# Expert layer: tokens routed and stored in four groups into a fixed region per expert, expert tiles fetched from computed addresses

## The chip, the core and the metric

The kernel runs on one core of a Trainium2 chip. The time is device time of one execution in microseconds (us), the median of several runs. Five engines work beside each other: TensorE (PE: matrix products; its weight loads show as PEld), VectorE (DVE), ScalarE (ACT), GpSimd (POOL) and SyncE (SP), which here only issues DMA transfers. They wait for each other by semaphores alone.

## The reference, cut to what matters

A stack of six layers over 64 x 32 = 2048 tokens of 256 numbers. Five of them (three kinds of attention, a ternary feed-forward layer and a gated attention) are left as they are. The sixth is a mixture of eight experts with a top-2 choice, whose inputs and weights are quantised:

```python
def activation_quant(x):                       # per token
    scale = 127.0 / jnp.maximum(jnp.max(jnp.abs(x), axis=-1, keepdims=True), EPS)
    return jnp.clip(jnp.round(x * scale), -128.0, 127.0) / scale
def expert_ffn(x, gw, uw, dw):                 # 256 -> 512 -> 256
    gate = bitlinear(x, gw)
    up = bitlinear(x, uw)
    activated = up * jnp.square(jax.nn.relu(gate))
    return bitlinear(activated, dw)
...
# last layer: x is normalised, a softmax over x @ router_w.T gives 8 probabilities a token,
# the two largest are kept and divided by their sum; the token's output is
# weight_1 * expert_1(x) + weight_2 * expert_2(x), and it is added to x
```

## The kernel before, in words

All layers stand in one program; each engine runs its own instruction list, layer after layer. The change is in the last layer, `experts` (L2437), and in one transfer of an earlier layer's list.

Tokens are held as 16 tiles of 128 (one token a partition). Each token goes to two experts, so 4096 rows have to be sorted by expert. Sorted, they fill at most `TILES` = 40 tiles of 128 rows, each of one expert, with blank rows at the end of an expert's last tile. The sorting goes through a table in device memory, `row_store`, of 40 x 128 rows of `ROW` = 132 words: 128 words hold the 256 quantised numbers as pairs of 16-bit floats, the last four the token's scale, its weight and the place its result goes to (`f_goes`). The stages are, with their engines:

- **Normalise and measure.** DVE normalises tile by tile (L165, `f_xn`) and takes each token's largest absolute value (L2657), from which the scales follow (L2663 to L2666). The whole of this comes first, for all 16 tiles.
- **Logits.** PE turns two tiles at a time (`turn_x`, L2798), ACT copies them out (`turned`, L2577), PE multiplies by the router's weights (`route`, L2806); all logits lie in one bank of PSUM.
- **Round and pack.** ACT rounds each tile to integers (`rounds`, L2582), POOL copies the low half words into `f_rows`, twice, since each token has two rows (L2550, 16 copies).
- **Route.** DVE takes softmax, ranks and choices of all 2048 tokens at once (L2681 to L2696, operations of 128 x 1024 among them), and "takes" of each token's two experts a value by multiplying by a mask and adding (`take`, L2699 and L2700). PE counts how many rows each expert gets and each row's rank within its expert (L2820 to L2824), with ACT's copy of the counts between (L2602). DVE makes of these counts the first tile of each expert, and from that each row's slot, `f_index`.
- **Store.** POOL issues 32 indirect DMAs (L2558), each of 128 rows to the slots that `f_index` gives; it waits ahead of the first for all copies, all scales, all indices and for the transfer that had written blank rows over the table (`f_blank_stored`; SP issues it at L857, in the second layer, on the queue that also brings the weights).
- **Fetch and compute.** SP waits for all 32 stores and then fetches the table in 20 sets of two tiles (L2532), up to six ahead. For each set PE turns the rows (`turn_in`, L2835), multiplies by up, gate and down weights whose place it reads from `f_owner_i` (L2878), ACT and DVE do what lies between, DVE takes the hidden rows' largest values and scales (L2747 to L2753), and POOL stores the results by indirect DMA (L2564, two a set) to `f_y_store`. At the end SP reads both results of each token back, they are added, and the output is stored.

SP, POOL and each compute engine do their list in order; a DMA issue that waits holds everything behind it on its engine. The lines of the kernel that the change touches:

## Time and profile before

| | |
|---|---|
| median of 3 runs (2062.59 to 2067.57) | 2063.86 us |
| the profiled execution: its own time | 2064.5 us |
| the profiled execution: span of the trace | 2061.7 us |
| mean granted TensorE clock | 0.924 |
| PE busy | 1688.7 us (82%) |
| DVE busy | 1586.4 us (77%) |
| ACT busy | 1190.8 us (58%) |
| POOL busy | 601.3 us (29%) |

Times in the trace count from the start of the span, so the last layer, which begins at about 1845 us, is read with times of 1845 to 2061.7. The busy shares are means over six layers; the change touches the last one alone, and what counts there is which wait ends last. The profiled execution's own time is 2.8 us above its span and 0.64 us above the median.

### The profile page before, as it was taken

To read this page: it belongs to the slowest core of one execution; us is meant where nothing else is said; L and a number is where in the kernel's file an instruction comes from. 1 tells how busy PE (TensorE), PEld (TensorE's weight loads), DVE (VectorE), ACT (ScalarE), POOL (GpSimd) and SP (SyncE) were. 2 spreads that over 40 slices of the span, in tenths; PEclk is the share of its full clock that TensorE was granted. 3 is DMA by queue.
4 is the path that set the end of the run, shared out by engine and by line. 5 is a ranking of instruction groups with operands and counts; after the bars stand their busy time and mean duration, and the time that the engine had idled before them with its cause. 6 is when DMAs were issued, how large, how long until landed. Compare 5 with 4: busy or idle time off the path is not lost.

```text
span 2061.7 us, 45477 instructions
## 1 busy us (share of the span) xinstructions
PE 1688.7 (82%) x13802; PEld 1240.8 (60%) x13802; DVE 1586.4 (77%) x4308; ACT 1190.8 (58%) x3322; POOL 601.3 (29%) x734
## 2 busy tenths in 40 slices
PE   6999999999999979766569898989899688862373
PEld 4677777777777758533357666666677566652241
DVE  5688888888888858789748878888887288873496
ACT  2555566556655636456427666676767466642493
POOL 0022222222222201011123434444433154435342
PEclk9999999999999999879779999999999789965797
DMA  2011111111111141020021222222111100000124
GB/s 97 15 33 29 29 29 29 29 29 29 30 32 29 43 107 24 32 79 1 3 70 43 62 62 62 62 62 62 41 32 33 25 14 12 12 11 20 52 76 154
DMA packets 119516, 87.10 MB, mean 42 GB/s; under 512 B 76992, under 2 KB 95747, under 8 KB 118661
## 3 DMA queue, kind: packets, MB, share of 16 engines
q1 hardware_dynamic: 116484, 79.71, 14.8%
q0 software_dynamic: 2944, 6.37, 0.9%
q8 instruction: 38, 0.62, 0.1%
q14 instruction: 50, 0.40, 0.1%
HBM read 72.05 MB, written 12.21 MB: 41 GB/s over the span
## 4 chain that ended last, share of the span: by engine, by line
PE 37%; DVE 30%; issue 15%; ACT 11%; POOL 2%; DVEq 1%; DMA 1%; ACTq 1%; SPq 1%; POOLq 0%
PE ps L669 3%; PE ps L1967 3%; PE ps L691 3%; PE ps L1895 3%; ACT a_pr L403 2%; DVE a_pT L532 2%; DVE a_nm L524 2%; PE ps L737 2%; DVE d_ks L1764 2%; PE ps L1946 2%; PE ps L1905 2%; PE ps L707 2%; ACT d_pr L1698 1%; POOL f_row_store L2558 1%; PE ps L1958 1%
## 5 line engine op out<-in xcount | busy, mean ns | idle before, releaser
L403 ACT ACTIVATE a_pr<-ps,a_nm 128x257 f32<-128x257 f32 x512 | 238.1, 473 | 174.3 <-DVE a_nm L524 174.3
L532 DVE COPY a_pT<-ps 128x512 f32<-128x512 f32 x256 | 170.3, 686 | 60.0 <-PE ps L707 59.5
L1718 ACT ACTIVATE d_pr<-d_st,d_nm 128x257 f32<-128x257 f32 x256 | 128.1, 502 | 128.7 <-DVE d_nm L1827 127.4
L330 POOL TENSOR_TENSOR a_sf<-a_sf,a_ratio 128x256 f32<-128x256 f32 x64 | 39.5, 616 | 474.1 <-DVE a_ratio L553 474.1
L524 DVE TENSOR_REDUCE a_nm<-ps 128x2 f32<-128x514 f32 x256 | 174.5, 681 | 0.0
L707 PE MATMUL ps<-ident,a_pr 128*128 128x128 f32 x1024 | 159.0, 278 | 0.0
L1946 PE MATMUL ps<-d_kc,d_qc 128*128 128x257 f32 x512 | 141.9, 400 | 14.7 <-DVE d_vc L1803 14.7
L1626 POOL TENSOR_TENSOR d_kc<-d_kc,d_ks 128x257 f32<-128x257 f32 x64 | 60.2, 941 | 266.4 <-ACT d_dist L1683 130.6
L707 PEld LDWEIGHTS ps<-ident,a_pr 128*128 128x128 f32 x1024 | 120.6, 143 | 25.7 <-issue 12.7
L669 PE MATMUL ps<-a_cT,a_wqk 128*128 128x257 f32 x512 | 132.7, 381 | 1.9 <-ACT a_v L393 0.8
L678 PE MATMUL ps<-a_wvg,a_cT 128*128 128x256 f32 x512 | 127.6, 392 | 0.0
L1631 POOL TENSOR_TENSOR d_qc<-d_qc,d_qs 128x512 f32<-128x512 f32 x64 | 94.2, 1472 | 81.6 <-DVE d_qs L1775 81.6
L1946 PEld LDWEIGHTS ps<-d_kc,d_qc 128*128 128x128 f32 x512 | 90.9, 191 | 42.9 <-DVE d_vc L1803 17.3
L1698 ACT ACTIVATE d_pr<-d_pr,d_ri 128x257 f32<-128x257 f32 x256 | 114.6, 497 | 0.0
L678 PEld LDWEIGHTS ps<-a_wvg,a_cT 128*128 128x128 f32 x512 | 92.0, 189 | 34.7 <-issue 24.8
L1823 DVE CUSTOM_DVE_ANT_0 d_st<-ps,d_wm 128x257 f32<-128x257 f32 x256 | 98.7, 424 | 15.1 <-issue 7.8
L691 PE MATMUL ps<-a_kT,a_qbd 32*128 32x289 f32 x1024 | 98.5, 453 | 13.2 <-ACT a_pr L403 10.3
L1691 ACT ACTIVATE d_pT<-ps 128x512 f32<-128x512 f32 x128 | 74.8, 584 | 59.0 <-PE ps L1932 58.9
L403 ACT ACTIVATION_READ_ACCUMULATOR a_pr<-ps,a_nm 128x1 f32 x512 | 103.0, 201 | 0.0
L669 PEld LDWEIGHTS ps<-a_cT,a_wqk 128*128 128x128 f32 x512 | 87.5, 191 | 10.1 <-ACT a_kT L388 1.3
L1958 PE MATMUL ps<-d_pT,d_vc 128*64 128x128 f32 x1024 | 85.1, 287 | 8.5 <-ACT d_pT L1691 7.8
L737 PE MATMUL ps<-a_pT,a_v 128*32 128x128 f32 x2048 | 82.5, 278 | 10.3 <-DVE a_pT L532 2.4
(385 smaller groups left out, 4400.3 us busy)
## 6 DMA issues: line engine op xcount, KB each, us to landing
a_cT<-in_ctx SPq DMA_DIRECT2D x64, 257.0 KB, 2.7
d_cT<-in_ctx SPq DMA_DIRECT2D x64, 257.0 KB, 2.8
f_wf<-in_f_w SPq DMA_DIRECT2D x24, 512.0 KB, 3.7
a_vbd<-a_vself SPq DMA_DIRECT2D x256, 8.0 KB, 1.8
d_lp<-d_pr SPq DMA_DIRECT2D x256, 0.5 KB
e_vb<-e_vs SPq DMA_DIRECT2D x256, 8.5 KB, 1.7
f_yab<-f_y_store SPq DMA_DIRECT2D x16, 256.0 KB, 5.5
c_wf<-in_c_w SPq DMA_DIRECT2D x3, 1024.0 KB, 7.2
```

Source lines behind the costliest of these rows:

```text
L403: ins = act.activation(pr[j][:, g, :], ps[:, S_BANK[u % 2] + k, S:LK], ACT.Exp, bias=nm[j][:, g:g + 1], accum_out=ssum[j][:, 0, g:g + 1])
L524: dve.tensor_reduce(nm[j][:, 2 * u:2 * u + 2], ps[:, s0:s0 + 2, S:LK], AX.X, ALU.max, negate=True).then_inc(max_ready.sem, 1)
L532: dve.tensor_copy(pT[u][:, :, :, :], ps[:, T_BANK[u % 2], :].rearrange("p (g c q) -> p g c q", g=2, c=2))\
L669: ins = pe.matmul(ps[:, P_BANK, 0:LC], lhsT=wqk[:, 1, k, m * P:m * P + P], rhs=cT[j][:, k, :], start=(k == 0), stop=(k == KT - 1))
L678: ins = pe.matmul(ps[:, P_BANK, c * HID:c * HID + HID], lhsT=cT[j][:, k, c * P:c * P + P], rhs=wvg[:, k, :], start=(k == 0), stop=(k == KT ...
L691: ins = pe.matmul(ps[:, g % HA, 0:LK], lhsT=qbd[j][rows(g), m, :, :].rearrange("p h q -> p (h q)"), rhs=kT[j][rows(g), m, :], start=True, ...
L707: ins = pe.transpose(ps[:, T_BANK[u % 2], (2 * k + c) * P:(2 * k + c + 1) * P], pr[j][:, 2 * u + k, c * P:c * P + P], ident[:, :])
L737: ins = pe.matmul(ps[rows(g), O_BANK, m * P:m * P + P], lhsT=v[j][:, c, g * S:g * S + S], rhs=pT[g // 2][:, g % 2, c, :], start=(m == 0 an ...
L1698: ins = act.activation(pr[j][:, g, :], pr[j][:, g, :], ACT.Copy, scale=ri[j][:, g:g + 1])
L1718: ins = act.activation(pr[j][:, g, :], st[u][:, k, :], ACT.Exp, bias=nm[u][:, k:k + 1], accum_out=sm[j][:, g:g + 1])
L1946: ins = pe.matmul(ps[:, S_BANK[u] + k, 0:LC], lhsT=qc[s // BT][:, g, s % BT, :, :].rearrange("p h q -> p (h q)"), rhs=kc[j][:, :], start=T ...
L1958: ins = pe.matmul(ps[KVC * k:KVC * k + KVC, O_BANK, u * P:u * P + P], lhsT=vc[j][:, c, :], rhs=pT[u][:, k, c, :], start=(u == 0 and c == 0 ...
```

## The change

- `row_store` has a fixed region of `REGION` = 16 tiles for each expert (and 8 tiles more): 136 tiles in place of 40. A row's slot is now its expert's region start (a constant, from the table `f_numbers`) plus its rank within the expert, which counts only the tokens up to it. The transfer of blank rows covers all 136 tiles.
- The 16 token tiles go in four groups of four. DVE's list is: normalise and measure groups 0 and 1, then for each group route, factors and places, followed by normalising the group two further on. Logits lie in four banks, PE counts and ranks group by group (`place_rows`), and POOL stores a group's eight indirect DMAs as soon as that group's index and scales are there.
- The packing into `f_rows` moves from POOL to ACT (`packed`).
- The 40 packed tiles are no longer contiguous in the table. After the last group DVE works out for each of the 40 tiles where it lies (`at_tile_i`), and SP fetches each tile by itself: it reads the number (`value_load`) and issues a DMA at that address. Ahead of the first it waits for this table besides the 32 stores.

```diff
+REGION = 16
+STORED = 8 * REGION + 8
...
-            eng.dma_start(row_store[:, :].rearrange("(k p) c -> p k c", p=P), spread(d["f_blank"], 1, TILES))\
+            eng.dma_start(row_store[:, :].rearrange("(k p) c -> p k c", p=P), spread(d["f_blank"], 1, STORED))\
...
+            stored = row_store[:, :].rearrange("(n p) c -> p n c", p=P)
+            eng.wait_ge(owner_ready.sem, owner_ready.at(0, 3))
...
-                eng.dma_start(tile_in[j][:, :, :], row_store[2 * u * P:2 * (u + 1) * P, :].rearrange("(k p) c -> p k c", k=2))\
-                    .then_inc(tile_loaded[u % 4].sem, 16)
+                for k in range(2):
+                    place_of = eng.value_load(at_tile_i[0:1, 2 * u + k:2 * u + k + 1], min_val=0, max_val=STORED - 1)
+                    eng.dma_start(tile_in[j][:, k:k + 1, :], stored[:, bass.ds(place_of, 1), :])\
+                        .then_inc(tile_loaded[u % 4].sem, 16)
...
-            for t in range(NT):
-                eng.wait_ge(rounded.sem, rounded.at(t, 1))
-                eng.tensor_copy(rows_h[:, :, t, 0:HID], spread(xn_low[:, t, 0:2 * HID:2], 1, 2)).then_inc(copied.sem, 1)
             eng.wait_ge(marked.sem, marked.at(0, 1))
-            eng.wait_ge(copied.sem, copied.at(NT, 0))
             eng.wait_ge(blank_stored.sem, blank_stored.at(1, 0))
-            eng.wait_ge(scales_ready.sem, scales_ready.at(0, 2))
-            eng.wait_ge(index_ready.sem, index_ready.at(0, 1))
-            for s in range(2):
-                for t in range(NT):
-                    eng.indirect_dma_start(row_store[:, :], bass.IndirectOffsetOnAxis(index[:, s, t:t + 1], 0),
-                                           rows[:, s, t, :], None).then_inc(rows_out.sem, 16)
+            for g in range(GROUPS):
+                eng.wait_ge(copied.sem, copied.at(GT * g + GT, 0))
+                eng.wait_ge(scales_ready.sem, scales_ready.at(g, 1))
+                eng.wait_ge(index_ready.sem, index_ready.at(g, 1))
+                for s in range(2):
+                    for t in range(GT * g, GT * g + GT):
+                        eng.indirect_dma_start(row_store[:, :], bass.IndirectOffsetOnAxis(index[:, s, t:t + 1], 0),
+                                               rows[:, s, t, :], None).then_inc(rows_out.sem, 16)
...
+            def packed(t):
+                act.wait_ge(rounded.sem, rounded.at(t, 1))
+                act.activation(rows_h[:, :, t, 0:HID], spread(xn_low[:, t, 0:2 * HID:2], 1, 2), ACT.Copy)\
+                    .then_inc(copied.sem, 1)
+
+            def exponents(g):
+                act.wait_ge(lg_in.sem, lg_in.at(g, 1))
+                act.activation(ex[:, GT * g:GT * g + GT, :], lg[:, GT * g:GT * g + GT, :], ACT.Exp).then_inc(lg_exp.sem, 1)
+
+            def counts_out(g):
+                act.wait_ge(count_psum.sem, count_psum.at(g, 1))
+                rows_of = GT * NE * (g + 1)
+                act.activation(counts16[0:rows_of, :], ps[0:rows_of, 3, 0:P], ACT.Copy).then_inc(count_ready.sem, 1)
...
+            for g in range(GROUPS):
+                act.wait_ge(size_ready.sem, size_ready.at(g, 1))
+                for t in range(GT * g, GT * g + GT):
+                    rounds(t)
+                if g < 3:
+                    turned(2 * g + 2)
+                    turned(2 * g + 3)
+                exponents(g)
+                for t in range(GT * g, GT * g + GT - 1):
+                    packed(t)
+                counts_out(g)
+                packed(GT * g + GT - 1)
...
+            def inputs(g):
+                for t in range(GT * g, GT * g + GT):
+                    normed(dve, xn[:, t, :], t).then_inc(xn_ready.sem, 1)
+                for q in (2 * g, 2 * g + 1):
+                    largest(q)
...
             rl = route_link
-            dve.wait_ge(lg_psum.sem, lg_psum.at(8, 0))
-            logits = ps[:, 2, 0:NT * NE].rearrange("p (t e) -> p t e", e=NE)
-            rl.link(dve, dve.tensor_reduce(top[:, :], logits, AX.X, ALU.max))
...
+                four = slice(GT * g, GT * g + GT)
+                dve.wait_ge(lg_psum.sem, lg_psum.at(2 * g + 2, 0))
+                logits = ps[:, LOGIT_BANK[g], GT * NE * g:GT * NE * (g + 1)].rearrange("p (t e) -> p t e", e=NE)
+                rl.link(dve, dve.tensor_reduce(top[:, four], logits, AX.X, ALU.max))
+                dve.tensor_tensor(lg[:, four, :], logits, spread(top[:, four], 2, NE), ALU.subtract).then_inc(lg_in.sem, 1)
...
+            def factors_of(g):
...
+                take(g, 1, spread(prob[:, four, :], 1, 2))
+                take(g, 2, spread(spread(ec[:, 0, :], 1, GT), 1, 2))
+                take(g, 3, spread(spread(ec[:, 1, :], 1, GT), 1, 2))
+                rl.link(dve, dve.tensor_tensor(tot[:, four], got[:, 1, 0, four], got[:, 1, 1, four], ALU.add))
+                rl.link(dve, dve.reciprocal(tot[:, four], tot[:, four]))
+                rl.link(dve, dve.tensor_tensor(got[:, 1, :, four], got[:, 1, :, four], spread(tot[:, four], 1, 2), ALU.mult))
+                dve.tensor_tensor(rows_f[:, :, four, ROW - 4], got[:, 2, :, four], spread(xs3[:, four], 1, 2), ALU.mult)
+                dve.tensor_tensor(rows_f[:, :, four, ROW - 3], got[:, 1, :, four], got[:, 3, :, four], ALU.mult)\
+                    .then_inc(scales_ready.sem, 1)
+
+            def places(g):
+                four = slice(GT * g, GT * g + GT)
+                dve.wait_ge(place_psum.sem, place_psum.at(g, 1))
+                rl.link(dve, dve.tensor_tensor(slot[:, four, :],
+                                               ps[:, 4, GT * NE * g:GT * NE * (g + 1)].rearrange("p (t e) -> p t e", e=NE),
+                                               spread(numbers[:, TILES:TILES + NE], 1, GT), ALU.add))
+                take(g, 0, spread(slot[:, four, :], 1, 2))
+                dve.tensor_copy(index[:, :, four], got[:, 0, :, four]).then_inc(index_ready.sem, 1)
+
+            inputs(0)
+            inputs(1)
+            for g in range(GROUPS):
+                route(g)
+                factors_of(g)
+                places(g)
+                if g + 2 < GROUPS:
+                    inputs(g + 2)
...
-            rl.link(dve, dve.scalar_tensor_tensor(slot[:, :, :], spread(first[:, :], 1, NT), float(P),
-                                                  ps[:, 4, 0:P].rearrange("p (t e) -> p t e", e=NE), ALU.mult, ALU.add))
-            take(0, spread(slot[:, :, :], 1, 2))
-            dve.tensor_copy(index[:, :, :], got[:, 0, :, :]).then_inc(index_ready.sem, 1)
...
+            rl.link(dve, dve.tensor_tensor(ended[:, :, :], ended[:, :, :], spread(spare[:, 0:NE - 1], 1, TILES), ALU.mult))
+            rl.link(dve, dve.tensor_reduce(at_tile[:, :], ended[:, :, :], AX.X, ALU.add))
+            dve.tensor_tensor(at_tile_i[:, :], at_tile[:, :], numbers[:, 0:TILES], ALU.add).then_inc(owner_ready.sem, 2)
...
+            def place_rows(g):
+                mine, upto = slice(GT * NE * g, GT * NE * (g + 1)), GT * NE * (g + 1)
+                pe.wait_ge(chosen_ready.sem, chosen_ready.at(g, 1))
...
+                pe.matmul(ps[0:upto, 3, 0:P], lhsT=chosen[:, 0:upto], rhs=ones16[:, :], start=True, stop=True)\
+                    .then_inc(count_psum.sem, 1)
+                pe.matmul(ps[:, 4, mine], lhsT=place16[:, 0:P], rhs=chosen[:, mine], start=True, stop=False)
+                pe.wait_ge(count_ready.sem, count_ready.at(g, 1))
+                ins = pe.matmul(ps[:, 4, mine], lhsT=counts16[0:upto, :],
+                                rhs=place16[0:upto, P + GT * NE * g:P + GT * NE * (g + 1)], start=False, stop=True)
...
-            for q in range(8):
-                if q < 7:
-                    turn_x(q + 1)
-                route(q)
-
-            chosen = chosen16[:, :, :].rearrange("p t e -> p (t e)")
-            pe.wait_ge(chosen_ready.sem, chosen_ready.at(0, 1))
-            pe.wait_ge(place_ready.sem, place_ready.at(0, 1))
...
+            for g in range(GROUPS):
+                place_rows(g)
+                if g + 2 < GROUPS:
+                    turn_x(2 * g + 4)
+                    turn_x(2 * g + 5)
+                    route(2 * g + 4)
+                    route(2 * g + 5)
```

On POOL, from the constant words to the first result stores, the list stood so before (names in brackets are the semaphores waited for: `pT_ready` is the packed copies, `both_hs_in_u_done_nxf_ready` the index, `both_hs_done_kn_ready_kf_ready` the scales, `oT_ready` the constant words):

```order
L2547 COPY f_rows<-f_goes 128x32x2 [waits w_loaded]
L2550 COPY f_rows<-f_xn 128x2x256 [waits ot_ready] x16
L2558 DMA f_row_store<-f_rows,f_index 5120x132 [waits both_hs_done_kn_ready_kf_ready,f_blank_stored,both_hs_in_u_done_nxf_ready,pT_ready,oT_ready]
L2558 DMA f_row_store<-f_rows,f_index 5120x132 x31
L2564 DMA f_y_store<-f_ys,f_tile_in 4096x256 [waits f_y_odd,f_y_even]
```

and after the change:

```order
L2555 MEMSET f_ones 128x128
L2557 COPY f_rows<-f_goes 128x32x2 [waits w_loaded]
L2566 DMA f_row_store<-f_rows,f_index 17408x132 [waits both_hs_done_kn_ready_kf_ready,pT_ready,both_hs_in_u_done_nxf_ready,f_blank_stored,oT_ready]
L2566 DMA f_row_store<-f_rows,f_index 17408x132 x7
L2566 DMA f_row_store<-f_rows,f_index 17408x132 [waits both_hs_in_u_done_nxf_ready,both_hs_done_kn_ready_kf_ready,pT_ready]
```

The 16 copies are gone from POOL, and the one wait ahead of 32 stores has become a wait ahead of each eight.

On DVE, at the end of the normalising, one routing of 16 tiles followed before:

```order
L2657 TENSOR_REDUCE f_am<-f_xn 128x2 [waits xn_ready] x2
L2663 TENSOR_SCALAR f_xs<-f_am 128x8 [waits max_ready]
L2664 RECIPROCAL f_xi<-f_xs 128x8 [waits f_size_link]
L2665 TENSOR_TENSOR f_xs<-f_xs 128x8
L2666 TENSOR_TENSOR f_xs<-f_xs 128x8 [waits f_size_link]
L2681 TENSOR_REDUCE f_top<-ps 128x16 [waits qk_psum,f_size_link]
L2682 TENSOR_TENSOR f_lg<-ps,f_top 128x128 [waits f_route_link]
L2684 TENSOR_REDUCE f_tot<-f_ex 128x16 [waits both_nhT_psum_ln_done]
L2685 RECIPROCAL f_tot<-f_tot 128x16 [waits f_route_link]
L2686 TENSOR_TENSOR f_prob<-f_ex,f_tot 128x128 [waits f_route_link]
```

and now, at the end of group 0's places (`L2722` and `L2723` are `take`, `pT_psum` the ranks from PE, `qk_psum` the logits), group 2's normalising stands between two routings:

```order
L2740 TENSOR_TENSOR f_slot<-ps,f_numbers 128x32 [waits pT_psum]
L2722 TENSOR_TENSOR f_picked<-f_pick,f_slot 128x2x32 [waits f_route_link]
L2723 TENSOR_REDUCE f_got<-f_picked 128x2x4 [waits f_route_link]
L2744 CAST f_index<-f_got 128x2x4 [waits f_route_link]
L167 TENSOR_SCALAR f_xn<-x_all,mv_all,rstd_all 128x256 x4
L2677 TENSOR_REDUCE f_am<-f_xn 128x2 [waits xn_ready] x2
L2683 TENSOR_SCALAR f_xs<-f_am 128x4 [waits max_ready]
L2684 RECIPROCAL f_xi<-f_xs 128x4 [waits f_size_link]
L2685 TENSOR_TENSOR f_xs<-f_xs 128x4
L2686 TENSOR_TENSOR f_xs<-f_xs 128x4 [waits f_size_link]
L2701 TENSOR_REDUCE f_top<-ps 128x4 [waits qk_psum,f_size_link]
L2702 TENSOR_TENSOR f_lg<-ps,f_top 128x32 [waits f_route_link]
```

The index of a group (L2744) now comes ahead of the normalising of the group two further on and of the next group's routing.

On SP, after the loads of the layer's small tables, the fetch of the first set was one instruction before:

```order
L2524 DMA f_lower<-in_f_lower 128x64
L2524 DMA f_place<-in_f_place 128x264
L2524 DMA f_numbers<-in_f_numbers 128x40
L2524 DMA f_goes<-in_f_goes 128x32
L2532 DMA f_tile_in<-f_row_store 128x2x132 [waits f_rows_out]
```

and is now, for the first set's first tile, with the beginning of the second's (`both_h_ready_exp_done` is the table of places):

```order
L2530 DMA f_numbers<-in_f_numbers 128x48
L2530 DMA f_goes<-in_f_goes 128x32
L2541 TENSOR_LOAD f_at_tile_i [waits f_rows_out,both_h_ready_exp_done]
L2541 ISA x2
L2542 ISA
L2542 DMA f_tile_in<-f_row_store 128x132
L2541 TENSOR_LOAD f_at_tile_i
```

Each tile's DMA has a load of its place and three register instructions ahead of it.

## Rows read from the trace of the kernel before

**Rows 1.** Windows; columns: us, busy PE (count), PEld, DVE, ACT, POOL, clock, DMA, GB/s.

```profile
1886.60:1930.80 44.20, 0.00 (x0) 0.02 (x1) 0.00 (x0) 0.00 (x0) 30.93 (x32) 0.50 0.17 56
1930.80:2036.00 105.20, 76.08 (x560) 45.86 (x560) 90.72 (x220) 87.66 (x140) 37.16 (x38) 0.95 0.21 64
```

**Rows 2.** Chain that ended last, in order of time; start us, us, what.

```profile
1885.41 0.23 DVE f_rows L2724
1886.64 1.24 POOL f_row_store L2558
...
1926.05 2.35 DMA f_row_store<-f_rows,f_index
1928.42 2.26 DMA f_tile_in<-f_row_store
1930.81 0.60 PE ps L2835 x4
```

**Rows 3.** Lines, POOL's row stores: ns min/median/max, first and last start.

```profile
L2558 POOL DMA_INDIRECT f_row_store<-f_rows,f_index x32: 954/958/1237, 1886.6 to 1926.1; - x32
```

**Rows 4.** Timeline, PE and ACT, logits and exponentials: start us, us, operation.

```profile
1853.05 1.71 PE L2806 MATMUL ps<-f_wr,f_xnT 128*128 128x8 f32 x8
...
1855.74 0.60 ACT L2577 ACTIVATE f_xnT<-ps 128x512 f32<-128x512 f32 x1 [1.86 <-PE ps L2798]
...
1868.63 1.28 ACT L2598 ACT_TABLE_LOAD   x1
1869.92 0.31 ACT L2598 ACTIVATE f_ex<-f_lg 128x128 f32<-128x128 f32 x1
```

**Rows 5.** Timeline, DVE, from normalising to the scales.

```profile
1847.72 1.38 DVE L165 TENSOR_SCALAR f_xn<-x_all,mv_all,rstd_all 128x256 f32<-128x256 f32 x4
...
1859.04 0.17 DVE L2666 TENSOR_TENSOR f_xs<-f_xs 128x8 f32<-128x8 f32 x1
...
1878.73 0.23 DVE L2694 TENSOR_SCALAR f_chosen<-f_rank 128x128 bf16<-128x128 f32 x1
...
1879.26 0.42 DVE L2699 TENSOR_TENSOR f_picked<-f_pick,f_prob 128x256 f32<-128x256 f32 x1
...
1881.08 0.21 DVE L2704 TENSOR_TENSOR f_rows<-f_got,f_xs 128x32 f32<-128x32 f32 x1
```

**Rows 6.** Timeline, POOL, packing copies.

```profile
1870.78 4.33 POOL L2550 COPY f_rows<-f_xn 128x512 f16<-128x512 f16 x4 [1.24 <-ACT f_xn L2582]
```

**Rows 7.** Timeline, POOL and DVE, one result store of an expert set.

```profile
1951.93 0.99 POOL L2564 DMA_INDIRECT f_y_store<-f_ys,f_tile_in  x1 [0.30 <-ACT f_ys L2632]
1952.31 0.16 DVE L2747 TENSOR_TENSOR f_ams<-f_ams,f_tile_in 128x2 f32<-128x2 f32 x1
1952.51 0.40 DVE L2748 TENSOR_SCALAR f_ams<-f_ams 128x2 f32<-128x2 f32 x1
```

**Rows 8.** Lines, DVE's small scale operations in the sets: ns min/median/max.

```profile
L2747 DVE TENSOR_TENSOR f_ams<-f_ams,f_tile_in x20: 161/161/163, 1939.4 to 2028.5; 128x2 f32<-128x2 f32 x20
L2748 DVE TENSOR_SCALAR f_ams<-f_ams x20: 168/261/404, 1939.6 to 2028.7; 128x2 f32<-128x2 f32 x20
```

**Rows 9.** Lines, PE's read of each tile's owner, and SP's fetches.

```profile
L2878 PEldq TENSOR_LOAD <-f_owner_i x40: 295/300/494, 1930.8 to 2019.8; - x40
L2878 PEldq FUSED_REGOPS  x40: 151/151/165, 1931.4 to 2020.2; - x40
...
L2532 SPq DMA_DIRECT2D f_tile_in<-f_row_store x20: 359/359/471, 1928.4 to 2016.1; - x20
```

**Rows 10.** Timeline of SP's queue: blank rows and the transfer after them.

```profile
755.70 0.62 SPq L857 DMA_DIRECT2D f_row_store<-in_f_blank  x1
870.48 0.34 SPq L1174 DMA_DIRECT2D d_wuq<-in_d_wuq  x1
```

**Rows 11.** DMA issues; KB, median us from issue to landing.

```profile
f_row_store<-in_f_blank SPq DMA_DIRECT2D x1, 2640.0 KB, 24.9
```

**Rows 12.** Window with the blank rows' transfer, columns as in rows 1.

```profile
770.00:780.00 10.00, 10.00 (x83) 8.36 (x81) 7.76 (x17) 4.93 (x14) 1.46 (x2) 1.00 1.15 173
```

## What was predicted

> **What bounds the kernel now.** The question is what the end of the last layer waits for, so the stage is read first. Between the first row store and the first matmul of the expert sets lie 44.2 us in which PE, DVE and ACT do nothing and POOL is busy for 30.9 [rows 1]. The chain of waits says why: DVE's scales end at 1885.64, POOL's first store starts 1.00 us later, POOL works through its list to the last store at 1926.05, whose transfer takes 2.35, then comes SP's fetch with 2.26 and PE's first matmul at 1930.81 [rows 2]. So the path is: routing of all 2048 tokens, then 32 stores, then the experts. The stores all take 0.96, at 39.4/31 = 1.27 us from start to start [rows 3]; the engine waits for nothing there, it is POOL's own pace. The sets behind take 105.2 us, with PE at 76, DVE at 91 and ACT at 88 [rows 1], and the change leaves their work as it is. What the change can move is the time of the last store, 1926.05, and what lies between it and the first matmul.
>
> **When the first group can be stored.** Slots no longer need the total counts, so group 0's index is ready after its own chain. Its logits end where they end now, at 1853.05 + 1.71 = 1854.76 [rows 4], since PE's list begins with the same turns. The exponentials wait on ACT behind the copy at 1855.74 (0.60), then a table load of 1.28, then at most 0.31: 1857.9 [rows 4]. (ACT's rounding of four tiles stands ahead as well; it fits into ACT's waits for PE there.) From there DVE runs a chain of dependent operations. Routing one group takes 128 x 32 and 128 x 256 shapes; the rows for these are 0.21 and 0.42 [rows 5]. Six small ones (1.26), five of 256 (2.1), three takes of two operations each, of 64 elements, at 0.25 between the two rows (3 x 2 x 0.25 = 1.5), five small ones for the factors (1.05) and the places with their take and cast (0.92) give 6.8. Index and scales of group 0: 1864.7. PE's ranks and ACT's copy of the counts lie beside DVE's factors. POOL begins 1.0 later as it does now [rows 2]: 1865.7, against 1886.64.
>
> **How fast the groups follow.** POOL needs 8 x 1.27 = 10.1 for a group. DVE needs, per group: normalising and measuring, now 11.5 us for 16 tiles (1847.72 to 1859.21 [rows 5]), with two more passes of four small operations at 0.17 (1.4 in all), so 12.85/4 = 3.2; the maximum, the subtraction and the wait for the exponentials, 0.7; and the 6.8: 10.7. Without friction DVE and POOL are nearly level.
>
> **Friction between POOL's stores and DVE.** DVE was idle during the row stores, so no row shows the two together here; the nearest are the result stores of the sets. While one runs (1951.93 to 1952.92), DVE's operation with one input from SBUF, L2748, takes 0.40 and ends with the store, though the operation with two inputs just before it, L2747, takes 0.16 under the same store [rows 7]. Over all 20 sets L2747 stays at 161 to 163 ns, while L2748 goes from 168 to 404 [rows 8]. So single-input elementwise operations wait for the store's end, others do not. A group has nine of them: four normalisations, one size, the choice, two picks, the cast. A store runs for 0.96 of each 1.27, so one that comes at random waits 0.76 x 0.48 = 0.37; nine wait 3.3, and POOL stores in 10.1 of about 13.2 us: 2.5. The bounds: 0, if the nine fall into the gaps; 5.5, if the four normalisations pass only one to a gap (4 x 1.27 - 1.4 = 3.7) and the other five wait 0.37 each. I take 2.5: nine times the longest stretch of L2748 (0.24) is 2.1, which is nearer to it than either end. Period: 13.2.
>
> The Trainium skill (SBUF — State Buffer, section "SBUF: two separate sides") says that DVE and GpSimd hold a shared port pair exclusively for a whole instruction, on DVE's side in a two-port mode or with two SBUF inputs when GpSimd reads SBUF. By its first half L2748 waits, which the trace agrees with; by its second L2747 would wait too, and 161 to 163 ns speak against that for this kind of POOL instruction. By the whole rule the time would be the second rival's, below.
>
> **The last store.** Group 2's index: 1864.7 + 2 x 13.2 = 1891.1. Group 3 has no normalising after it and is ready about 9.4 later, inside the 10.1 in which POOL stores group 2. So POOL works through 16 stores from 1891.1 + 0.95, and the last begins 15 x 1.27 = 19.05 later, at 1911.1 instead of 1926.05: **15.0 us earlier**. With the bounds of friction: 1906.1 (20.0 earlier) and 1917.1 (9.0 earlier).
>
> **The fetch.** A tile's DMA now has a load of its place and three register instructions ahead. The trace shows no such load on SP; PE's read of the owner is the nearest, 0.30 and 0.15 [rows 9], and an issue on SP takes 0.36 [rows 9]. PE needs both tiles of the first set, whose second DMA begins 2 x (0.30 + 0.15) + 0.36 + gaps = 1.4 later than the one DMA now: **-1.4**, between 1.0 and 1.8 if the loads take the 0.49 of the slowest. The half-sized transfers may take less than 2.26, which I leave at nothing. In the sets SP needs some 0.95 a tile, 1.9 a set, while a set takes (2028.5 - 1939.4)/19 = 4.7 [rows 8], with six sets fetched ahead: hidden. The Trainium skill (DMA: Bandwidth & Descriptors, "Latency and other measured facts") gives about 600 ns as the floor of such a load; at that price the time would be 0.6 higher, and no row of SP shows it yet.
>
> **What costs nothing, and under which cover.** POOL's 16 copies (4.33 for four shown, the rest alike [rows 6]) lay beside DVE's routing, so their leaving gains nothing; on ACT, 16 copies of 512 elements at 0.60 [rows 4] add 2.4 to a group, which with rounding, turning and the exponentials stays near 6.3 of 13.2. If ACT had no such room it would cost up to 2.4 a group. The table of places at the end of DVE's list is some 3.3 us beside POOL's last stores; uncovered it would cost those 3.3. The blank rows grow from 2640 to 8976 KB: they go at 2640/24.9 = 106 KB a us [rows 11], so 84.7 us from 755.70, to about 840, before SP's next transfer at 870.48 [rows 10]; even with the transfers queued ahead, PE is busy for 10.00 of 10 us there while the DMA engines are full [rows 12], and nothing waits for these rows before 1865. If they went below 78 KB a us they would reach into the next layer's weights.
>
> **Sum.** 2064.5 - 15.0 + 1.4 = 2050.9 for an execution like the profiled one; this lies 0.64 above the median of the runs, so 2050.3 against 2063.86.
>
> **Rivals.** (a) No friction: POOL and DVE run level, period 10.7, last store at 1906.1, 2064.5 - 20.0 + 1.4 = 2045.9, on the median's base 2045.3. For it: the gaps between stores are 0.3 and most of DVE's operations are shorter. Against: L2748's end at the store's end.
>
> (b) DVE is locked out: its operations with two SBUF inputs wait as well. Then of a group's eight stores 7.7 us are lost to it, less the 2.2 in which it reduces or reads PSUM: +5.5 on every group, period 16.2, and the last group, without normalising, takes 13.0. Last index 1864.7 + 32.4 + 13.0 = 1910.1, last store 1.0 + 7 x 1.27 later at 1920.0, only 6.1 earlier: 2064.5 - 6.1 + 1.4 = 2059.8, or 2059.2. L2747 speaks against it [rows 8], but those are two numbers a partition, not 256.
>
> (c) Slower: SP's fetches set the pace of the sets. This decides from 4.7/2 = 2.35 us a tile on; at 3.0, 40 x 3.0 = 120 against 94 us for the sets costs 26 and eats the gain: 2064.5 - 15.0 + 26 = 2075.5, or 2074.9. The rows on PE and SP add up to 0.95 [rows 9], so the loads would have to be several times dearer on SP.
>
> (d) The groups do not overlap: if something in a group's chain waits for the previous group's stores, the last group ends where the routing ends now and nothing is gained: about 2064.
>
> **How the numbers follow.** Forecast 0.70, (a) 0.12, (b) 0.11, (c) 0.04, (d) 0.03. The range 2044.5 to 2057.5 takes in the forecast with both bounds of friction (9.0 earlier gives 2056.3) and of the fetch, and (a): 0.82 of the chance. A measurement of this kernel tells about 0.3% from no change, that is 6.2 us, 2057.7 and 2070.0. The forecast and (a) lie below: faster 0.82; (b) and (d) within: 0.14; (c) above: 0.04.
>
> **What would show it.** In the profile after: the first row store near 1865.7; starts of the 9th, 17th and 25th store some 13 apart, the 25th right behind the 24th; DVE's normalisations of groups 2 and 3 stretched from 0.35 towards 1.27, its products of two inputs not; the last store near 1911; PE's first matmul of the sets 6.2 after it instead of 4.8; SP's loads of places near 0.3; sets at 4.7 as now. The forecast is wrong where DVE's products stretch under a store (then b), where the first index comes much later than 1865 because a wait on ACT or PE holds group 0, or where the sets grow longer behind SP's list.

## The result and the profile after

The median went from 2063.86 us (7 runs, 2060.19 to 2067.57) to 2050.17 us (7 runs, 2039.92 to 2053.15): a ratio of 0.993, with a 95% interval of 0.9916 to 0.9945. The forecast was 2050.3. The profiled execution of after took 2053.15 us, the longest of the seven, with a span of 2051.4 us and a mean granted clock of 0.927; against the profiled execution of before that is 10.3 us of span. One of the seven runs, 2039.92, lies 6 us below the next; it was not traced, but its mean granted clock was 0.935, where the other six had 0.926 to 0.929.

The time agrees with the sum better than the parts do. Two of its terms were wrong by about as much, in opposite directions: the stores came 6 us earlier than forecast, and the expert sets, which were to stay as they were, became 7.5 us longer.

**The stores.** The first lines of this timeline (start us, us, operation, idle time before and what ended it) answer to [rows 2, 3]; of the 32 stores the 1st, 9th, 17th, 25th and last are shown.

```profile
1866.46 1.41 POOL L2566 DMA_INDIRECT f_row_store<-f_rows,f_index  x1 [17.65 <-DVE f_index L2744]
...
1877.01 0.96 POOL L2566 DMA_INDIRECT f_row_store<-f_rows,f_index  x1 [0.30 <-issue]
...
1887.33 0.96 POOL L2566 DMA_INDIRECT f_row_store<-f_rows,f_index  x1 [0.31 <-ACT f_rows L2595]
...
1897.42 0.96 POOL L2566 DMA_INDIRECT f_row_store<-f_rows,f_index  x1 [0.30 <-issue]
...
1906.26 0.96 POOL L2566 DMA_INDIRECT f_row_store<-f_rows,f_index  x1 [0.30 <-issue]
```

After the first store POOL never waits again: every store follows its predecessor by 0.30 us. The groups start 10.55, 10.32 and 10.09 us apart; the forecast had 13.2. It is a near thing: the indices of groups 1 and 2 end 1.23 and 1.19 us ahead of their groups' first stores, and POOL, when it stood idle ahead of group 0, began 0.98 us after the index. POOL sets the pace by some 0.2 us. The normalising began 1.15 us later in this execution (1848.87 against 1847.72; 0.9 of it is there already at the loads of the third layer's weights, which SP issues just ahead of the blank rows, and between the profiled executions of the ten kernels here this start lies anywhere from 1844.78 to 1849.72), so the last store lies 57.4 us after the normalising's start, where it lay 78.3 before and was forecast at 63.4.

**DVE beside the stores.** The timeline of DVE, answering to [rows 5]: a group that is normalised before any store, one beside stores, and the four casts of the index.

```profile
1848.87 1.38 DVE L167 TENSOR_SCALAR f_xn<-x_all,mv_all,rstd_all 128x256 f32<-128x256 f32 x4
...
1859.07 0.18 DVE L2704 TENSOR_REDUCE f_tot<-f_ex 128x4 f32<-128x32 f32 x1 [2.62 <-ACT f_ex L2600]
...
1865.31 0.17 DVE L2744 CAST f_index<-f_got 128x8 int32<-128x8 f32 x1
...
1875.61 0.17 DVE L2744 CAST f_index<-f_got 128x8 int32<-128x8 f32 x1
1875.69 1.43 DVE L167 TENSOR_SCALAR f_xn<-x_all,mv_all,rstd_all 128x256 f32<-128x256 f32 x4
...
1885.97 0.17 DVE L2744 CAST f_index<-f_got 128x8 int32<-128x8 f32 x1
...
1893.00 0.30 DVE L2744 CAST f_index<-f_got 128x8 int32<-128x8 f32 x1
```

Four normalisations took 1.38 us in quiet and 1.43 beside stores; the indices end 10.30, 10.36 and 7.16 us apart. The same routing with no store beside it (the kernel that waits for all groups, below) has its last index 44.29 us after the start of the normalising; here it is 44.43. The friction forecast at 2.5 us a group is 0.14 us over all four, nearly all of it in the last cast, 0.30 us instead of 0.17.

**The sets.** The windows answer to [rows 1] (us, busy PE, PEld, DVE, ACT, POOL, clock, DMA share, GB/s): from the first to the last turning of a set.

```profile
1912.70:2009.40 96.70, 71.58 (x494) 42.34 (x495) 79.98 (x194) 78.09 (x125) 29.53 (x30) 0.92 0.22 63
```

Before, the same stretch (1930.81 to 2019.94) took 89.1 us. PE's turnings show where the rest is: three of the twenty waited for the fetch of their tiles, which none did before.

```profile
1941.74 0.40 PE L2894 MATMUL ps<-identh,f_tile_in 128*128 128x128 f16 x4 [1.95 <-DMA f_tile_in<-f_row_store]
...
1962.70 0.40 PE L2894 MATMUL ps<-identh,f_tile_in 128*128 128x128 f16 x4 [0.57 <-DMA f_tile_in<-f_row_store]
...
1993.73 0.40 PE L2894 MATMUL ps<-identh,f_tile_in 128*128 128x128 f16 x4 [0.75 <-DMA f_tile_in<-f_row_store]
```

The chain of waits shows what stands before the first of the three (start us, us, what; the short steps between are left out):

```profile
1933.52 2.43 DMA f_y_store<-f_ys,f_tile_in
...
1936.02 0.28 SPq L2541
...
1936.75 0.34 SPq L2542
...
1937.13 0.27 SPq L2541
...
1937.84 3.85 DMA f_tile_in<-f_row_store
1941.69 0.05 issue
1941.74 0.40 PE ps L2894 x4
```

The seventh set goes into the buffer of the first, so SP waits for the first set's results to land (1935.95). Then it reads a place, issues a DMA, reads the second place and issues the second DMA at 1937.84, 1.9 us after it could start. PE would have turned that set one period (4.75) after 1934.84, at 1939.6, that is 3.65 us after the buffer came free; the second tile is there 5.74 us after it.

Two things add up in this. The first is the longer way: the wait, two reads and two issues. The second is in the trace's records of single transfers. A fetch lands in 16 parts; 15 parts of this one were there at 1939.67, 1.83 us after its issue, like other fetches here (median 1.8), and the last at 1941.69. From 1938.60 to 1940.21 a 16 KB load of instructions ran; the queue of these loads, in the stretch from 1938.50 to 1940.30 (packets, MB, share of 16 engines):

```profile
q8 instruction: 1, 0.02, 5.6%
```

Without that last part the fetch would have been complete 3.72 us after the buffer came free, where PE wanted it after 3.65: the longer way had used up the slack, and the load made a wait of it. For the other two late sets the late part is one of the results that free the buffer, beside loads at 1956.22 and 1987.91. The chain before the third:

```profile
1986.31 3.70 DMA f_y_store<-f_ys,f_tile_in
...
1991.90 1.78 DMA f_tile_in<-f_row_store
1993.73 0.40 PE ps L2894 x4
```

Of this store of results 15 parts had landed 2.42 us after the issue, the last one 3.70 after it. In the five kernels here with six buffers and both places read behind the wait, 16 turnings are shown waiting for a refetch, and each comes 2.4 to 6.7 us after the start of such a load; the loads themselves come 14 to 18 us apart, and not every one makes a set late. That the late part stood behind the load on its DMA engine is inferred from the times; the records do not name the engine, and no run takes a load away.

**The whole difference**, on the two profiled executions: 1.15 later start, stores 20.9 earlier by the stage's own clock (78.3 - 57.4), last store to first matmul 6.48 instead of 4.76 (+1.7), sets +7.5, the end of the layer +0.3: -10.3. The blank rows cost nothing that shows: their transfer is three times as large, and SP's next issue comes 115.0 us after it, as before (114.8, [rows 10]).

```profile
756.44 0.65 SPq L859 DMA_DIRECT2D f_row_store<-in_f_blank  x1
871.41 0.33 SPq L1176 DMA_DIRECT2D d_wuq<-in_d_wuq  x1
```

### The profile page after: what moved, and what is told of

Same layout as the page of the kernel before. It is cut to its first block, busy times and chain, and to the rows that moved or that the text cites. A ratio compares the mean times of both kernels' runs of the same rounds, so it can differ in the third digit from the quotient of the medians.

```text
span 2051.4 us, 45828 instructions
## 1 busy us (share of the span) xinstructions
PE 1697.1 (83%) x13811; PEld 1245.1 (61%) x13811; DVE 1599.8 (78%) x4404; ACT 1199.2 (58%) x3344; POOL 589.9 (29%) x718
## 4 chain that ended last, share of the span: by engine, by line
PE 37%; DVE 30%; issue 15%; ACT 11%; POOL 2%; DMA 2%; DVEq 1%; SPq 1%; ACTq 1%; POOLq 0%
PE ps L671 3%; PE ps L1969 3%; PE ps L693 3%; PE ps L1897 3%; ACT a_pr L405 2%; DVE a_pT L534 2%; DVE a_nm L526 2%; PE ps L739 2%; DVE d_ks L1766 2%; PE ps L1948 2%; PE ps L1907 2%; PE ps L709 2%; ACT d_pr L1700 1%; PE ps L1960 1%; PE ps L627 1%
## 5 line engine op out<-in xcount | busy, mean ns | idle before, releaser
L671 PEld LDWEIGHTS ps<-a_cT,a_wqk 128*128 128x128 f32 x512 | 87.5, 191 | 10.1 <-ACT a_kT L390 1.3
```

The source lines that it names most:

```text
L671: ins = pe.matmul(ps[:, P_BANK, 0:LC], lhsT=wqk[:, 1, k, m * P:m * P + P], rhs=cT[j][:, k, :], start=(k == 0), stop=(k == KT - 1))
```

## The experiments

Two questions stood open: what made the sets longer (theory A: the refetch comes too late for six buffers; theory B: the split transfers slow the sets), and which part of the change carries the gain. All kernels but one are edits of the changed kernel.

### Eight buffers

```diff
-        HELD = 6
+        HELD = 8
```

> The changed kernel with eight buffers for fetched sets instead of six, nothing else. Theory A (late refetch): in the changed kernel the refetch of a set takes 5.7 us from the landing of the results that free its buffer to the landing of its second tile, against 3.65 us until PE wants it, and three such lateness stalls made the sets 7.5 us longer; with two more sets of buffers the fetch starts two sets (9.5 us) earlier and the stalls go: first to last turning of the sets 89 to 90 us instead of 96.6, time about 2043. Theory B (split transfers): two half-sized DMAs beside the result stores slow the sets themselves whatever the buffers: time stays at 2050, sets stay at 96 us.

Measured: 2043.92 us (6 runs; ratio to before 0.9909, 0.9893 to 0.9924), 6.3 below the changed kernel's median. PE's waits in the sets, first after the change (engine, line, what it waited for: us in total, times, longest), then here:

```profile
PE ps L2894 <- DMA f_tile_in<-f_row_store: 25.3, 4, 22.0
```

```profile
PE ps L2894 <- DMA f_tile_in<-f_row_store: 22.1, 1, 22.1
```

The one wait that is left is the wait ahead of the first set; the three in the sets are gone, and the first to last turning takes 88.6 us. Theory A holds, theory B falls: the split transfers are all there. The loads of instructions are there too: the last part of a result store at 1963.97 landed after 3.76 us, and with two more buffers no set waits for it.

The windows explain why 3.3 us of waiting (1.95 + 0.57 + 0.75) had cost 7.5. In the changed kernel, the period before the first late set, that set, and the two sets after it:

```profile
1936.00:1941.70 5.70, 3.36 (x24) 1.96 (x24) 5.53 (x14) 5.07 (x9) 1.97 (x2) 1.00 0.25 74
1941.70:1948.20 6.50, 5.34 (x29) 2.92 (x30) 3.83 (x10) 3.43 (x5) 3.38 (x4) 0.74 0.22 63
1948.20:1957.00 8.80, 6.87 (x57) 4.50 (x56) 7.67 (x17) 7.88 (x14) 2.52 (x3) 1.00 0.21 61
```

and with eight buffers, from the second set to the last turning:

```profile
1914.60:1998.00 83.40, 61.73 (x472) 38.21 (x478) 79.17 (x190) 75.74 (x122) 29.41 (x30) 1.00 0.24 69
```

After PE's wait the granted clock is 0.74 over the next period, between its two levels (1.2 and 2.4 GHz), and that set takes 6.5 us instead of 4.75; the other two late sets read 0.73 over 6.3 us each. Without the waits the clock stays at 1.00. That it is the clock and not the wait that lengthens the set is seen in the kernel with early exponentials (below), where one set that had waited 0.66 us kept the full clock and one that had waited 0.61 did not:

```profile
1957.10:1961.80 4.70, 3.56 (x28) 2.25 (x29) 4.48 (x12) 3.56 (x6) 1.97 (x2) 1.00 0.27 85
...
1986.60:1993.00 6.40, 5.23 (x28) 2.88 (x29) 4.85 (x12) 4.37 (x8) 2.35 (x3) 0.73 0.20 62
```

### Places read ahead of the waits

```diff
-            eng.wait_ge(rows_out.sem, rows_out.at(2 * NT, 0))
             for u in range(SETS):
                 j = u % HELD
+                places_of = [eng.value_load(at_tile_i[0:1, 2 * u + k:2 * u + k + 1], min_val=0, max_val=STORED - 1)
+                             for k in range(2)]
+                if u == 0:
+                    eng.wait_ge(rows_out.sem, rows_out.at(2 * NT, 0))
...
                 for k in range(2):
-                    place_of = eng.value_load(at_tile_i[0:1, 2 * u + k:2 * u + k + 1], min_val=0, max_val=STORED - 1)
-                    eng.dma_start(tile_in[j][:, k:k + 1, :], stored[:, bass.ds(place_of, 1), :])\
+                    eng.dma_start(tile_in[j][:, k:k + 1, :], stored[:, bass.ds(places_of[k], 1), :])\
```

> The changed kernel with SP reading both tiles' places ahead of its waits (for the stores and for the free buffer), so that only two DMA issues follow each wait. Theory A: the second DMA of a set starts 0.4 us after the wait instead of 1.9, so the first refetch lands about 4.2 us after the results instead of 5.7, late by 0.6 us against PE's 3.65 instead of 2.1; the sets lose 1 to 3 us instead of 7.5 and the first matmul comes 1.6 us earlier: about 2044 (2042 to 2047). Theory B: only the 1.6 us ahead of the first set are saved: about 2048.5.

Measured: 2042.52 us (6 runs; 0.9906, 0.9892 to 0.9921), at the faster end of theory A's range. Its sets do better than expected, where 1 to 3 us were to be lost: no turning is shown waiting, first to last turning 89.3 us, with six buffers as before. The chain from the last store to the first set:

```profile
1903.51 2.29 DMA f_row_store<-f_rows,f_index
...
1905.99 0.35 SPq L2544
...
1906.53 1.88 DMA f_tile_in<-f_row_store
1908.40 0.14 issue
1908.54 0.60 PE ps L2896 x4
```

The second DMA starts 0.73 us after the stores' landing, and the first matmul 5.03 us after the last store instead of 6.48. The expectation had kept the 3.85 us of the late transfer, which is not the price of a fetch: in this kernel the fetches land in 1.7 to 1.9 us. The refetch of the seventh set is issued at 1932.34 and 1932.86 and has landed by 1934.68, 0.09 us before the next load of instructions begins (1934.77). The results that free the next buffer are delayed by it, and that set's fetch lands 0.05 us ahead of its turning: with six buffers little is left even so.

### Eight buffers in the kernel before

```diff
-        HELD = 6
+        HELD = 8
```

> The kernel before with eight buffers for fetched sets. Theory A: one DMA issued at once after the wait lands within 2.4 to 3.6 us, inside PE's 3.65, so more buffers change nothing: within 1.5 us of before. Theory B': the buffers were already too few before the change: 2 us or more faster.

Measured: 2063.14 us (12 runs; 0.9999, 0.9986 to 1.0011). The interval alone would leave room for a gain of 2 us or a little more. The trace of before decides: no turning but the first waits for a fetch, and each of its refetches lands 0.14 to 1.63 us ahead of the turning (median 1.4). Six buffers were enough for one DMA issued at once; it is the change that made them too few.

### All groups waited for before the first store

```diff
+            eng.wait_ge(index_ready.sem, index_ready.at(GROUPS - 1, 1))
             for g in range(GROUPS):
                 eng.wait_ge(copied.sem, copied.at(GT * g + GT, 0))
```

> The changed kernel with POOL waiting for the last group's index ahead of its first store; the groups and fixed regions stay, only the overlap of stores and routing goes. If the overlap carries the gain: the last index comes at 1893.2, then 1 us and 31 x 1.265 us to the last store at 1933.4 instead of 1906.3: 27 us longer, about 2077. If the gain came from elsewhere (slots without total counts, packing on ACT): about 2050 to 2064.

Measured: 2076.22 us in a single run, 26 above the changed kernel's median. POOL's first and last store:

```profile
1890.11 1.42 POOL L2567 DMA_INDIRECT f_row_store<-f_rows,f_index  x1 [45.58 <-issue]
...
1929.69 0.96 POOL L2567 DMA_INDIRECT f_row_store<-f_rows,f_index  x1 [0.31 <-issue]
```

The indices of the first and of the last group, with no store beside the routing:

```profile
1861.24 0.17 DVE L2745 CAST f_index<-f_got 128x8 int32<-128x8 f32 x1
...
1888.90 0.17 DVE L2745 CAST f_index<-f_got 128x8 int32<-128x8 f32 x1
```

The last index ends at 1889.07, the stores begin 1.0 us later and take their 39.6 us. The last store lies 84.9 us after the start of the normalising (1844.78 in this trace), against 57.4 with the overlap and 78.3 before. Routing in groups alone is thus 6.6 us slower than routing at once; the overlap gives 27.5 us.

### Packing given back to POOL

```diff
             for g in range(GROUPS):
+                for t in range(GT * g, GT * g + GT):
+                    eng.wait_ge(rounded.sem, rounded.at(t, 1))
+                    eng.tensor_copy(rows_h[:, :, t, 0:HID], spread(xn_low[:, t, 0:2 * HID:2], 1, 2))\
+                        .then_inc(copied.sem, 1)
                 eng.wait_ge(copied.sem, copied.at(GT * g + GT, 0))
...
-                for t in range(GT * g, GT * g + GT - 1):
-                    packed(t)
                 counts_out(g)
-                packed(GT * g + GT - 1)
```

> The changed kernel with the packing given back to POOL: four copies of 1.08 us stand in POOL's list ahead of each group's eight stores. If POOL is the pace of the stores: a group takes 4.3 + 10.1 = 14.4 us on POOL instead of 10.1; group 0's copies lie before its index, so three times 4.3 = 13 us are added, last store near 1919 instead of 1906.3 (counted as in the changed kernel's trace), time about 2063; the gain is gone. If POOL has room for them, because the groups' indices come only every 10.3 us: within 3 us of 2050.

Measured: 2061.91 us in a single run. The last store lies 64.7 us after the start of the normalising (1913.41 - 1848.68), 7.3 later than in the changed kernel, where 13 were expected. POOL is the pace, as the first theory says, but a copy is cheaper here (ns min/median/max, first and last start):

```profile
L2563 POOL COPY f_rows<-f_xn x16: 603/613/802, 1853.1 to 1903.7; 128x512 f16<-128x512 f16 x16
```

Three groups at 4 x 0.61 are 7.3 us. The 1.08 a copy of [rows 6] were taken beside DVE's operations of 128 x 1024; the other 12 copies of that trace took 0.57 to 0.62 us. Against the changed kernel's profiled execution (2053.15) this run is 8.8 us longer: these 7.3, and 1.6 between the last turning and the end; the sets took 96.4 us against 96.6. By the last store more than half of the gain is gone, by the run against the median more than that.

### First exponentials early

```diff
                 if g < 3:
                     turned(2 * g + 2)
+                if g == 0:
+                    exponents(g)
+                if g < 3:
                     turned(2 * g + 3)
-                exponents(g)
+                if g > 0:
+                    exponents(g)
```

> The changed kernel with ACT's first exponentials (and with them the table load of 1.28 us) ahead of the second copy of turned tokens instead of behind it; nothing else. DVE waited 2.62 us for them in group 0. If everything behind hangs on the first index: exponentials at 1856.7 instead of 1859.0, all four groups and the last store 2.3 us earlier, time about 2048. If the later groups' own pace (ACT, PE) takes the place of it: less than 1 us.

Measured: 2048.54 us (6 runs; 0.9928, 0.9914 to 0.9943), 1.6 below the changed kernel's median, whose interval and this one's overlap. The trace is clearer: ACT's table load and exponentials,

```profile
1852.10 1.28 ACT L2600 ACT_TABLE_LOAD   x1
1853.48 0.23 ACT L2600 ACTIVATE f_ex<-f_lg 128x32 f32<-128x32 f32 x1
```

now lie beside DVE's work, the first index ends 14.3 us after the start of the normalising instead of 16.6, and the last store lies 55.1 after it instead of 57.4. Both moved by 2.3 us: the stores hang on the first index.

### Copies on DVE beside the stores

```diff
+                for t in range(GT * g, GT * g + GT):
+                    dve.tensor_copy(yab[:, t, 0, :], x_all[:, t, :])
                 for q in (2 * g, 2 * g + 1):
                     largest(q)
```

> The changed kernel with four plain copies of 128x256 floats from SBUF to SBUF added on DVE to each group's normalising (they write a buffer that is not in use yet), to measure the friction by itself: groups 0 and 1 are normalised before any store runs, groups 2 and 3 beside stores. Theory C (an operation in DVE's fast mode waits for a store's end if it falls into its last 0.4 us, others never wait): a copy takes about 0.2 us in groups 0 and 1, some of those in groups 2 and 3 reach 0.4 to 0.6, the normalisations stay at 0.35 everywhere; time 1 to 4 us longer. Theory D (no friction at all on this kind of store): copies alike in all groups, 0.8 us longer a group. Theory E (as predicted, every single-input operation waits wherever it falls): copies up to 1.2 us and normalisations stretched with them.

Measured: 2051.59 us in a single run. The copies of groups 0 and 1 (no store runs), of group 2 (beside the first store) and of group 3, each four together; then the first three stores:

```profile
1847.76 0.89 DVE L2692 COPY f_yab<-x_all 128x256 f32<-128x256 f32 x4
...
1851.84 0.89 DVE L2692 COPY f_yab<-x_all 128x256 f32<-128x256 f32 x4
...
1864.74 0.89 DVE L2692 COPY f_yab<-x_all 128x256 f32<-128x256 f32 x4
...
1875.90 1.02 DVE L2692 COPY f_yab<-x_all 128x256 f32<-128x256 f32 x4
```

```profile
1864.52 2.21 POOL L2566 DMA_INDIRECT f_row_store<-f_rows,f_index  x1 [18.13 <-DVE f_index L2746]
1867.04 0.96 POOL L2566 DMA_INDIRECT f_row_store<-f_rows,f_index  x1 [0.30 <-issue]
1868.30 0.96 POOL L2566 DMA_INDIRECT f_row_store<-f_rows,f_index  x1 [0.30 <-issue]
```

One of the eight copies beside stores is longer, 0.40 us instead of 0.28, at the end of the store that runs from 1875.87 to 1876.83; four normalisations take 1.42 instead of 1.38. Theory E, the prediction's, falls. Of C and D the trace favours C: what is stretched lies at a store's end. The first store is the one that pays, 2.21 us instead of 1.41. The Trainium skill (SBUF — State Buffer, section "SBUF: two separate sides") warns that a plain copy of fp32 within SBUF on DVE keeps GpSimd from writing a DMA's descriptors; this store agrees, but the store that ran beside group 3's copies kept its 0.96. The last store lies 59.3 us after the start of the normalising, 1.9 later than without the copies: DVE's indices now come 11.1 and 11.4 us apart, slower than POOL's 10.1.

### Eight buffers, early reading and early exponentials together

```diff
-        HELD = 6
+        HELD = 8
...
+                places_of = [eng.value_load(at_tile_i[0:1, 2 * u + k:2 * u + k + 1], min_val=0, max_val=STORED - 1)
+                             for k in range(2)]
...
+                if g == 0:
+                    exponents(g)
```

> The changed kernel with eight buffers, both places read ahead of the waits, and ACT's first exponentials early. If the three act on different stretches: 7.5 (sets) + 1.7 (first set) + 2.3 (first index) = 11.5 less than the changed kernel, about 2039. If eight buffers and early reading do the same thing twice, as theory A says of the sets, but each has its own place otherwise, the same 2039; if the first index no longer counts, 2041.

Measured: 2038.17 us (5 runs; ratio to before 0.9876, 0.9859 to 0.9893), 12 us below the changed kernel and the fastest here. The profiled execution of it was a longer one (2046.49). Its normalising began at 1849.72, 3.8 us later than in that of eight buffers alone, and its sets took 91.8 us, 3.2 more. No set waits in it; its first three sets show where these 3.2 are, in the clock:

```profile
1909.90:1915.00 5.10, 3.60 (x12) 1.61 (x14) 0.20 (x1) 1.91 (x3) 0.00 (x0) 0.50 0.20 55
1915.00:1920.50 5.50, 3.91 (x13) 1.60 (x12) 4.07 (x11) 3.03 (x5) 0.00 (x0) 0.50 0.31 76
1920.50:1926.00 5.50, 4.77 (x21) 2.48 (x20) 4.09 (x10) 4.03 (x6) 0.00 (x0) 0.50 0.21 50
```

With eight buffers alone the clock had risen to 1.00 with the second set.

## Why the prediction was right, and where only its sum was

- **What bounds the stage** (POOL's row of stores behind the routing): right. Waiting for all groups gives 27.5 us back, and POOL's own copies show at once in the last store. DVE is only some 0.2 us off that path, though: the two are nearly level, as the working without friction said.
- **First index at 1864.7, first store at 1865.7**: right. 16.6 us after the start of the normalising against 17.0 forecast (1864.7 - 1847.72); 17.6 against 18.0 for the store. DVE's wait for the exponentials (2.62) was the longest wait in it, and with early exponentials the 2.3 us gained there reach the last store in full.
- **Period 13.2**: wrong; the step is the friction. The uncontended 10.7 was nearly right (10.3), the 2.5 a group for waits behind stores are 0.14 over all four. The failing step is "single-input elementwise operations wait for the store's end", made from L2748 [rows 7, 8]. In all 17 sets of before in which a result store ran, L2748 started 0.58 to 0.83 us into it: the row only ever saw a store's last 0.4 us (with eight buffers it once started 0.38 into a store and took its quiet 0.17). The routing's choices and picks at 1882.54 to 1882.89 lie at 0.28 to 0.63 of a store and take their quiet 0.17 to 0.18 each; the cast at 1893.00, 0.62 into a store, is stretched to the store's end. So in these traces only the last 0.4 us of a store delay DVE, and not every operation: of the last four normalisations the one that began 0.58 into a store took 0.47 us instead of 0.40, the others did not change. Rival (a), with a chance of 0.12, described the stores: last store 58.4 us after the start of the normalising (1906.1 - 1847.72), 57.4 measured. Rival (b) is refuted for these stores: DVE's products of two SBUF inputs took 0.42 or 0.43 us in every group. They thus do not show the lock for a whole instruction that the Trainium skill states (SBUF — State Buffer, "SBUF: two separate sides").
- **Fetch -1.4**: nearly right, -1.7. A place's load took 0.27 us at the median and 0.49 for the first, near PE's rows. The Trainium skill (DMA: Bandwidth & Descriptors, "Latency and other measured facts") gives about 600 ns as the floor; here the 0.27 counts.
- **Sets unchanged, fetches hidden behind six buffers**: wrong, 7.5 us. The working asked for SP's throughput (0.95 a tile against 2.35) and not for the way from a freed buffer to the turning: "six sets fetched ahead" holds only until the first refetch. A buffer comes free when its results have landed (1935.95 for the first), and by then PE had turned the sixth set (1934.84): nothing was left ahead, and the refetch had what remained of one period. The rows for it were in the trace of before: results stored at 1951.93 [rows 7], landed 2.4 us later, the next turning of that buffer at 1958.04, a fetch of 2.1 to 2.6 us between. Eight buffers and early reading each remove the stalls alone; eight buffers in the kernel before show that it had none to remove. Which sets were late was decided by loads of instructions, as far as the times show it. More than half of the loss (4.2 of 7.5) is not the 3.3 us of waiting but PE's clock after it, which no term held.
- **Blank rows, table of places, packing**: right at nothing. The kernel with POOL's copies shows that the packing's move was needed although its time lay off the path before: in the new order it would stand in POOL's list between the stores. One reading of it was wrong: of the 16 copies of before, the four shown were the slow ones, not like the rest.
- **The sum**: -15.0 + 1.4 was forecast. By the stage's own clock it was -20.9 + 1.7 + 7.5 + 0.3 = -11.4 in the profiled execution; the medians give -13.7. That the time came out at the forecast is in part luck. The range held because it was wide enough for (a).

## What to carry to other kernels

Where a transfer is moved to computed addresses, look at the shortest way from "buffer free" to "data wanted", not at the queue's throughput: loads of addresses belong ahead of the wait, and a longer way needs more buffers (either gave 6 to 8 us here). A way without slack turns each late part of a transfer into a wait. Where one engine's list of equal pieces sets the pace, cut the work before it into groups so that it starts early, keep everything else out of its list, and shorten the way to the first group, which counts in full. A row of two engines meeting prices only the part of the operation in which they met: look where in it each meeting fell before the price is put on every operation.

## What the hardware showed

- PE's clock fell to 0.73 or 0.74 on the mean of the period after waits of 0.57 to 1.95 us in the sets, which made that set 1.5 to 1.7 us longer than 4.75. Not every such wait did it: in the kernel with early exponentials waits of 1.33 and 0.66 us left the clock at 1.00, and one of 0.61 was followed by 0.73.
- At the start of the sets the clock rose from 0.50 to 1.00 with the second set in some executions, with the third or the fourth in others; where it was the fourth (all three improvements together), two sets took 5.6 us instead of 3.9 and 4.2.
- A row store on POOL took 0.96 us, the first of a row 1.41, and 2.21 where DVE copied beside it. Why the first is longer stays open.
- While a 16 KB load of instructions ran (0.9 to 1.6 us), single parts of fetches and result stores landed up to 2 us after the other 15: 3.85 us instead of 1.83 for a fetch, 3.70 instead of 2.42 for a store.
